# A graph layer's edge loop: its small transfers and index copies made in batches of eight, four and two groups

## The reference, cut to what matters

```
h   = relu(layernorm(x))
msg = relu(concat(h[src], h[dst], w) @ W1 + b1) @ W2 + b2     # one row for each edge
agg = segment_max(msg, dst)                                   # 0 where a node has no edge
x   = x + relu(concat(h, agg) @ U1 + c1) @ U2 + c2
h   = relu(layernorm(x))
x   = x + relu(h @ root + segment_sum(proj[src, rel_type], dst) + bias)
```

## Time and profile before

| what | value |
|---|---|
| time, median of 3 runs | 8358.6 us (8357.57 to 8365.55) |
| span of the one profiled execution | 10613.5 us |
| busy in it: PE / PEld / DVE / ACT / POOL | 6874.5 / 5005.1 / 4445.3 / 959.0 / 6076.6 us |
| first layer's edge loop in it | 151.3 to 5486 us |
| second layer's edge loop in it | 5630.5 to 10581 us |

### The profile page before, as it was taken

One profiled execution on the slowest core, in us unless ns is written; L12 is line 12 of the kernel. 1 busy time (PEld: TensorE's weight loads), 2 busy tenths in 40 slices (PEclk: granted clock), 3 DMA queues, 4 the chain that ended last, 5 costly groups with the idle time before them and its releaser, 6 DMA issues. The chain is left out here.

```text
span 10613.5 us, 125396 instructions
## 1 busy us (share of the span) xinstructions
PE 6874.5 (65%) x29078; PEld 5005.1 (47%) x29078; DVE 4445.3 (42%) x10997; ACT 959.0 (9%) x1738; POOL 6076.6 (57%) x6284
## 2 busy tenths in 40 slices
PE   5767767677677776767675666555656655565656
PEld 3444444444444444444444555444545545454545
DVE  5444444444444444444453343334433433433434
ACT  2100100001000101000021000000000000000001
POOL 2555555555555555555535666666666666666665
PEclk8777777777777777777787777777777777777777
DMA  5222222222222222222232111111111111111112
GB/s 150 74 73 74 72 73 72 73 74 74 73 71 73 72 74 71 74 71 73 72 80 56 42 41 42 42 42 41 42 41 42 41 42 41 42 41 42 41 42 58
DMA packets 415228, 646.13 MB, mean 61 GB/s; under 512 B 128130, under 2 KB 232010, under 8 KB 414451
## 3 DMA queue, kind: packets, MB, share of 16 engines
q0 software_dynamic: 200704, 411.44, 15.7%
q1 hardware_dynamic: 214482, 234.24, 7.6%
HBM read 617.04 MB, written 28.13 MB: 61 GB/s over the span
## 5 line engine op out<-in xcount | busy, mean ns | idle before, releaser
L575 POOL DMA_INDIRECT G<-p_tab,idxs x3136 | 2984.3, 952 | 2441.4 <-DVE idxs L661 1463.1
L1065 POOL DMA_INDIRECT hT<-h_tab,idxs x3136 | 3090.7, 986 | 1849.4 <-issue 911.9
L1082 PE MATMUL psA<-S,hT 128*128 128x256 f32 x6272 | 2131.4, 498 | 1748.4 <-DVE S L1149 1374.1
L1082 PEld LDWEIGHTS psA<-S,hT 128*128 128x128 f32 x6272 | 1490.2, 250 | 2079.1 <-issue 935.2
L678 DVE TENSOR_TENSOR_SCAN R<-mk,R,psM 128x512 f32<-128x512 bf16 x784 | 998.5, 1274 | 1671.2 <-issue 760.0
L603 PE MATMUL psM<-Z,w 128*128 128x512 f32 x1568 | 1115.0, 801 | 855.3 <-ACT Z L649 712.0
L1159 DVE TENSOR_TENSOR aggT<-psV,aggT 128x64 f32 x784 | 174.8, 223 | 2889.2 <-remote 1451.7
L619 PE MATMUL psE<-E,O 128*128 128x64 f32 x6272 | 1025.8, 319 | 406.7 <-DVE E L689 338.3
L1092 PEld LDWEIGHTS psV<-A,V 128*128 128x128 f32 x6272 | 1007.9, 231 | 411.9 <-issue 175.6
L619 PEld LDWEIGHTS psE<-E,O 128*128 128x128 f32 x6272 | 973.2, 237 | 484.2 <-DVE E L689 390.4
L1092 PE MATMUL psV<-A,V 128*128 128x64 f32 x6272 | 969.1, 308 | 273.5 <-ACT A L1110 144.9
(11 more groups left out here) (86 smaller groups left out, 2611.9 us busy)
## 6 DMA issues: line engine op xcount, KB each, us to landing
mk<-marks SPq DMA_DIRECT2D x392, 256.0 KB
G<-p_tab,idxs POOLq DMA_INDIRECT x3136
pl<-marks SPq DMA_DIRECT2D x392, 128.0 KB
hT<-h_tab,idxs POOLq DMA_INDIRECT x3136
Qw<-q_tab SPq DMA_DIRECT2D x784, 32.0 KB
p_tab<-pq SPq DMA_DIRECT2D x14, 448.0 KB, 3.1
q_tab<-pq SPq DMA_DIRECT2D x14, 448.0 KB, 4.1
oh<-in_w SPq DMA_DIRECT2D x392, 4.0 KB
```

Source lines behind the costliest of these rows:

```text
L575: pool.indirect_dma_start(G[:, s, j, :], None, p_tab, bass.IndirectOffsetOnAxis(ap=idxs[:, s, j:j + 1], axis=0)).then_inc(gathered[s], 16)
L1065: pool.indirect_dma_start(G[:, s, j, :], None, h2_tab, bass.IndirectOffsetOnAxis(ap=idxs[:, s, j:j + 1], axis=0)).then_inc(l1_gathered[s], 16)
L1082: ins = nc.tensor.matmul(psA[:, b, 0:NB * W], G[:, s, j, :], S[:, b, j, :, :].rearrange("p b w -> p (b w)"), start=j == 0, stop=j == GT - 1)
```

## The change

A pass of the loop now holds 16 groups (GPB) instead of 8; 49 passes in all. Rings of 8 slots (RING) stay for `G`, `Qw` and `oh`. In `max_edges`:

- `marks` come for eight groups at once, in two buffers, ordered eight groups ahead; `pl` and `mk` are as large as before in all.
- SP loads eight row numbers at once and then brings four windows and the weights of four groups together (`quad`), once PE has used the four groups whose places they take.
- `indices` copies the indices of eight groups with one instruction, in every eighth step, behind that step's `scan`. `idx_ready` counts eights.
- `onehot` forms two groups with one instruction (64 x 1024 elements).
- `E` is formed for two groups with one instruction (`lasts`), ahead of `picks`.
- DVE loads eight row numbers at once for `add`.
- PE, ACT and POOL do the same work with fewer waits. POOL still issues four indirect transfers for each group.

```diff
+GPB = 16
+RING = 8
+QUAD = 4
...
+        def windows(eng, kind, table, at, n):
+
+            _, rows = nc.values_load_multi_w_load_instructions(
+                table[0:1, bass.ds(at, n)], engines=[kind], min_val=0, max_val=NP,
...
+            return rows
...
-                E = sb("E", [P, 2, GT, W], fp32)
-                pl = sb("pl", [WQ, GPI // 2, HALF], bf16)
-                mk = sb("mk", [P, GPI // 2, HALF], bf16)
-                idxs = sb("idxs", [P, GPI, GT], i32)
+                E = sb("E", [P, 2, 2 * GT, W], fp32)
+                pl = sb("pl", [WQ, GPB // RING, OCT], bf16)
+                mk = sb("mk", [P, GPB // RING, OCT], bf16)
+                idxs = sb("idxs", [P, GPB, GT], i32)
...
+                        def marks_in(k, h):
+
+                            sp.dma_start(pl[:, h, :], marks[0, bass.ds(k * GE, OCT)].partition_broadcast(WQ)
+                                         ).then_inc(places_loaded[h], 16)
+                            sp.dma_start(mk[:, h, :], marks[1, bass.ds(k * GE, OCT)].partition_broadcast(P)
+                                         ).then_inc(masks_loaded[h], 16)
+
+                        def quad(i, s, rows, tails):
+                            k, r = GPB * i + s, s % RING
+
+                            if there(k - RING):
+                                sp.wait_ge(z_done, k - RING + QUAD)
+                                sp.nop(nofuse=True)
+                            for n in range(QUAD):
+                                sp.dma_start(Qw[0:W, r + n, :], q_tab[bass.ds(rows[r + n], W), :]).then_inc(windows_loaded[s // QUAD], 16)
...
+                            sp.dma_start(oh[WQ:WQ + 1, r:r + QUAD, :].rearrange("p a e -> p (a e)"),
+                                         row(w)[:, bass.ds(k * GE, QUAD * GE)]).then_inc(windows_loaded[s // QUAD], 16)
...
+                            quad(i, s, rows, tails)
+                            if isinstance(k, int) and k == 0:
+                                marks_in(0, 0)
+                            quad(i, s + QUAD, rows, tails)
+                            if not (isinstance(k, int) and k + RING >= NGRP):
+
+                                if there(k - RING):
+                                    sp.wait_ge(scanned, k + 1)
+                                    sp.nop(nofuse=True)
+                                marks_in(k + RING, 1 - s // RING)
...
-                            pool.wait_ge(idx_ready, k + 1)
-                            pool.nop(nofuse=True)
-                            if there(k - GPI):
-                                pool.wait_ge(z_done, k - GPI + 1)
+                            k = GPB * i + s
+                            if s % RING == 0:
+                                pool.wait_ge(idx_ready, (GPB // RING) * i + s // RING + 1)
+                                pool.nop(nofuse=True)
+                            if there(k - RING):
+                                pool.wait_ge(z_done, k - RING + 1)
                                 pool.nop(nofuse=True)
...
+                        def indices(i, h):
+
+                            s = h * RING
+                            k = GPB * i + s
+                            if there(k - GPB):
+                                for n in range(s, s + RING):
+                                    dve.wait_ge(gathered[n], 16 * GT * i)
+                            dve.nop(nofuse=True)
+                            nc.vector.tensor_copy(idxs[:, s:s + RING, :].rearrange("p s j -> p (s j)"),
+                                                  idx0[:, bass.ds(k * GT, RING * GT)]).then_inc(idx_ready, 1)
...
-                            nc.vector.tensor_scalar(oh[0:WQ, s, :], pl[:, s // 2, b * GE:(b + 1) * GE], place[0:WQ, 0:1], None,
+                            nc.vector.tensor_scalar(oh[0:WQ, r:r + 2, :].rearrange("p a e -> p (a e)"),
+                                                    pl[:, s // RING, r * GE:(r + 2) * GE], place[0:WQ, 0:1], None,
                                                     ALU.is_equal).then_inc(onehot_ready, 1)
...
+                        def lasts(k, r):
+
+                            if there(k - 4):
+                                dve.wait_ge(picked, k - 2)
+                            dve.nop(nofuse=True)
+                            nc.vector.tensor_tensor(E[:, r // 2, :, :], lane[:, :].unsqueeze(1).to_broadcast([P, 2 * GT, W]),
+                                                    relL[:, bass.ds(k * GT, 2 * GT)].unsqueeze(2).to_broadcast([P, 2 * GT, W]),
+                                                    ALU.is_equal)
...
                         def step(i, s):
-                            k = GPI * i + s
-                            if not (isinstance(k, int) and k + HOT >= NGRP):
-                                onehot(i + (s + HOT) // GPI, (s + HOT) % GPI)
-                            if not (isinstance(k, int) and k + AHEAD >= NGRP):
-                                indices(i + (s + AHEAD) // GPI, (s + AHEAD) % GPI)
+                            k = GPB * i + s
+                            if s % RING == 0:
+                                skip = 3 if isinstance(k, int) and k == 0 else 0
+                                dve.nop(nofuse=True)
+                                got = windows(dve, mybir.EngineType.DVE, win, k - 3 + skip, RING - skip)
+                                for n in range(skip, RING):
+                                    rows[s + n] = got[n - skip]
+                            if s % 2 == 0 and not (isinstance(k, int) and k + HOT >= NGRP):
+                                onehot(i + (s + HOT) // GPB, (s + HOT) % GPB)
                             if there(k - 1):
-                                scan(i - (s == 0), (s + GPI - 1) % GPI)
+                                scan(i - (s == 0), (s + GPB - 1) % GPB)
+                            if s % RING == 0 and not (isinstance(k, int) and k + RING >= NGRP):
+                                indices(i + s // RING, 1 - s // RING)
                             if there(k - 2):
+                                if s % 2 == 0:
+                                    lasts(k - 2, (s + 2) % 4)
                                 picks(k - 2, s % 2)
                             if there(k - 3):
-                                add(k - 3, (s + 1) % 2)
+                                add(k - 3, (s + 1) % 2, rows[s])
```

More of the change, by code:

```diff
@@ L499, in _, with rounds @@
                         pool.sem_clear(s)
+        def windows(eng, kind, table, at, n):
+            _, rows = nc.values_load_multi_w_load_instructions(
+                table[0:1, bass.ds(at, n)], engines=[kind], min_val=0, max_val=NP,
+                skip_runtime_bounds_check_because="a window starts at a node and is moved no further than the last row")
+            return rows
         def max_edges(tag, again, wide=False):
             WQ = W + wide
+            BLKS = NGRP // GPB
+            OCT = RING * GE
+            assert NGRP % GPB == 0 and BLKS >= 3
+            def rounds(eng, step):
+                for s in range(GPB):
+                    step(0, s)
+                with eng.Fori(1, BLKS - 1) as i:
+                    for s in range(GPB):
+                        step(i, s)
+                for s in range(GPB):
+                    step(BLKS - 1, s)
             with ExitStack() as ph:
                 sb, ps = tensors(ph, tag)
-                G = sb("G", [P, GPI, GT, D], fp32)
-                Qw = sb("Qw", [WQ + 1, GPI, D], fp32)
-                oh = sb("oh", [WQ + 1, GPI, GE], fp32)
+                G = sb("G", [P, RING, GT, D], fp32)
+                Qw = sb("Qw", [WQ + 1, RING, D], fp32)
+                oh = sb("oh", [WQ + 1, RING, GE], fp32)
                 Z = sb("Z", [P, 2, GE], fp32)
@@ L563, in _ @@
-                        sweep(sp, step)
+                            rows = windows(sp, mybir.EngineType.SP, win, k, RING)
+                            tails = windows(sp, mybir.EngineType.SP, row(last), k, RING) if wide else None
+                            quad(i, s, rows, tails)
[5 more added lines that the diff above has]
+                                    sp.wait_ge(scanned, k + 1)
+                                    sp.nop(nofuse=True)
+                                marks_in(k + RING, 1 - s // RING)
@@ L565, in _ @@
+                        rounds(sp, step)
                     @block.gpsimd
@@ L705, in _ @@
                         dve.wait_ge(place_ready, 1)
-                        for s in range(HOT):
-                            onehot(0, s)
+                        onehot(0, 0)
                         dve.wait_ge(consts_loaded, 48)
@@ L721, in step @@
                                 picks(k - 2, s % 2)
                             if there(k - 3):
-                                add(k - 3, (s + 1) % 2)
-                        sweep(dve, step)
-                        scan(ITERS - 1, GPI - 1)
+                                add(k - 3, (s + 1) % 2, rows[s])
```

(4 more changed lines are left out.)

126 lines of the change are left out of this document (50 added, 76 removed).

## The result

The changed kernel takes 8445.9 us (median of 4 runs, 8444.0 to 8459.9), the kernel before beside it 8358.7 (4 runs, 8357.6 to 8365.6): ratio 1.0106 [1.0094, 1.0119], 87.2 us slower. The forecast, 8384, had the sign and 25 of these 87 us; its range ended at 8420.

What follows compares the result with a forecast made beforehand. POOL's indirect transfers, 1.25 us each and 5.0 us a group, were taken to set the pace of both loops. To 8358.6 us came +25 for longer one-hot holds and 0 for all else: 8384 us, range 8335 to 8420.

Steps and rivals of the forecast that it cites:

- The ledger: POOL's idle time in both loops: 2250 us of real waits, taken off the 10613.5 us span, leave 8363 us.
- the waits belong to the profiled execution: Both loops: in timed runs POOL hardly ever waits; the 2250 us of waits occur only in the profiled execution.
- E was put at nothing: DVE's E for two groups: 0.67 us a pair, hidden behind POOL's 5.0 us a group; no holds assigned to it.
- the one-hots' base: First loop's gathers: 19 us of extensions by single one-hots, 26 us if POOL were always at work.
- the memset's 5: The gather of 5.80 us beside the 10.6 us memset, read as the large case of the hold: 4.9 us.
- square law: Gathers beside one-hots: cost grows with hold length squared; pairs cost 1.8 to 2.8 times singles, +21 to +48 us.
- its 0.37 us: A gather beside a one-hot: POOL shut out for 0.09 + 0.28 us from the one-hot's start; pairs 0.70 to 0.88.
- Marks: Marks loaded for eight groups: 1.5 MB at once, landing near 12.8 us, wanted after 30 us; 0 us.
- The index copy: DVE's index copy by eights: 779 copies become 98, saving DVE 120 us off the path; slack 27 us, 0 us.
- Rival 1: First loop's gathers: longer holds fall where DVE doesn't touch the port; 8358 us, bounds 8342 to 8375, chance 0.38.
- Rival 2: POOL waits in timed runs; the deeper index lead removes it: 8301 to 8244 us; chance 0.12 including small gains.
- Rival 3: A late window or mark stalls PE: 98 us if once in eight groups at 1 us, 8457 us; chance 0.04.

Runs made afterwards that it cites:

- b3: The kernel before, unchanged, profiled again in the short condition: gathers of the first loop mean 965 ns; timed 8376.6 us beside e7b.
- e5: The changed kernel with E for two groups reading `lane` from PSUM instead of SBUF: 10156.6 us, 0.9576 of the kernel before, long condition.
- e6: The changed kernel with one-hot pairs formed by a slower three-input operation, one input in PSUM: 10106.6 us, 0.9530 of the kernel before, long condition.
- e4: The changed kernel with one-hots and E for one group again: 10137.4 us, 0.9540 of the kernel before, long condition.
- a1: The changed kernel, unchanged, run again in the long condition: 10192.7 us, 0.9612 of the kernel before.
- e2: The changed kernel with one-hots for one group again, E still in pairs: 10165.4 us, 0.9569 of the kernel before, long condition.
- e7b: The changed kernel with one-hot pairs and E pairs each taking one input from PSUM, short condition: 8318.6 us, 0.9931 of the kernel before.

## Why the prediction came out short

**The ledger was right as arithmetic and wrong as a reading.** Span less POOL's waits is the time of the short condition, to 0.05%, and in after POOL waits 2.7 us, with gaps of 0.305. But "the waits belong to the profiled execution" was false. They belong to a condition that timed runs have too. The conclusion that POOL sets the pace holds for the result, since the time to be predicted was of the short one.

**The step that failed: E was put at nothing, and the one-hots' base was too small.** The prediction gave all holds to the one-hots: 19 us of them (24 less the memset's 5), scaled to 26, and a factor of 1.8 to 2.8. Each gather that is held ends one of two fixed times after the end of one DVE instruction (below), so its excess can be put to that instruction. Counted over the mean of the gathers that nothing stretches (946.0 ns in b3, 943.6 in after), in us:

| held by | before (long) | b3 (short) | after (short) | after less b3 | in the prediction |
|---|---|---|---|---|---|
| one-hots | 9 | 42 | 85 | +43 | 26 to 51, +25 |
| E | 11 | 11 | 67 | +56 | nothing |
| memset's gather | 5 | 5 | 0 | -5 | 0 |

*E.* It is the larger part, +56 us, nearly the 62 us that the forecast fell short. In the trace that the prediction had, E already held about half of it; it read one gather beside a one-hot and gave the rest to the one-hots too, without a reason. e5 and e6 show both parts by leaving out: 58 us for E and 62 for the one-hots, of 114. Here the Trainium skill had the missing half on the page the prediction cited ("SBUF — State Buffer", section "SBUF: two separate sides"): the pair of ports is also locked by a DVE operation with two inputs in SBUF, against a GpSimd operation that reads SBUF. The trace agrees: E is such an operation, the gather reads `idxs`, and with `lane` in PSUM its share goes.

*The one-hots' base* was counted where POOL was standing. In the long condition the index copy comes right behind the one-hot and POOL waits for that copy, so POOL is mostly not at a gather's start while a one-hot runs. Scaling by POOL's busy share, 3920 of 5313, takes the two as independent, and they aren't: in before, 318 of 778 one-hots start in one of POOL's waits, which fill 28% of the time, and 75 are under way when a gather begins; in b3, without waits, 425 of 780 are. The base is 42 us, not 26. The factor for them, 85/42 = 2.0, is in the prediction's range.

**The factor, and what a hold is.** In the long condition pairs over singles give 2.5 (e4 to a1); in the short one 152 of after stand to 50 of b3, 3.0. The prediction had 1.8 to 2.8 by a square law on a hold read from one pair of rows, and took the lower end; the one-hots alone have 2.0, E alone 6. Sorted by where the DVE instruction starts, seen from the start of the gather that overlaps it alone, the records of both kernels give one law (ns):

| instruction, kernel | starts at | gathers | mean excess | its end less the excess |
|---|---|---|---|---|
| one-hot of 2, after | -550 to -500 | 42 | 87 | 125 |
| | -350 to -300 | 15 | 286 | 126 |
| | -150 to -100 | 57 | 483 | 124 |
| | -50 to 50 | 14 | 0 | |
| | 200 to 250 | 7 | 142 | 820 |
| | 350 to 400 | 11 | 288 | 821 |
| | 550 to 900 | 148 | 0 | |
| E of 2, after | -400 to -350 | 76 | 160 | 127 |
| | 50 to 100 | 30 | 468 | |
| | 300 to 350 | 38 | 0 | |
| one-hot of 1, b3 | -350 to -300 | 38 | 24 | 126 |
| | -150 to -100 | 73 | 224 | 125 |
| | 0 to 350 | 185 | -1 | |
| | 400 to 450 | 9 | 77 | 824 |

A gather wants something that DVE holds at two moments, 0.125 and 0.82 us after its start. If a one-hot that began at least 0.1 us ahead of the gather (an E: 0.02) is still running at the first, the gather waits for its end. At the second it waits for a one-hot that began less than 0.47 us into it, never for an E. The row "50 to 100" of E is a mixture. In 24 of its 30 gathers the index copy of eight groups runs across the first moment, as in the timeline above, and 23 of them wait to the end of the E behind it, 0.61 us; the six without the copy wait for nothing. In e5, with the same copy there and `lane` in PSUM, 14 such gathers lose 0.014 to 0.022 us, to the copy's end. So the index copy in eights isn't free: together with E it brings 14 of E's 67 us.

These rules give all but some 3 us of what is held in after and in b3. They are of these two kernels, these two instructions and the short condition. In the long one they leave more open: in e2 five gathers beside an E that starts 0.32 us after them are held 0.85 us (the longest 1803 ns), and in e6 15 us of 56 follow neither moment. The hold also goes the other way. A one-hot that starts 0.55 to 0.7 us into a gather ends 1.455 us after the gather's start wherever in that stretch it began (44 in after), 0.715 and its usual 0.74; in b3 15 of them end at 1.19, 0.715 and 0.475.

For the first moment a one-hot's useful length is its own less 0.22 us. A single one-hot has a quarter of a microsecond left (0.475 - 0.22), a pair has 0.51. For the second, a single one that starts 0 to 0.34 us into the gather is over before 0.82, a pair is not. Met at any phase of 1.25 us, the one-hots would cost 784 x (0.25^2/2 + 0.125^2/2) / 1.25 = 24 us as singles and 392 x (0.51^2/2 + 0.39^2/2) / 1.25 = 65 as pairs; E by the first moment alone 784 x 0.27^2/2 / 1.25 = 23 and 392 x 0.53^2/2 / 1.25 = 44. Together 47 and 109, an estimate with a factor of 2.3; measured 50 and 152.

By kind the estimate is up to twice off either way: 24 and 65 against 42 and 85 for the one-hots, 23 and 44 against 11 and 67 for E. That rest is phase, which the law of squares leaves out: 57 pairs of one-hots start in the costliest 50 ns, and 118 of the 392 E pairs start 0.72 to 0.9 us into a gather, from where 0.67 us reach past the first moment of the next and 0.42 would not. The change set both the length and the phase, and no run in the short condition separates them.

The prediction read its 0.37 us (0.09 ahead and 0.28 of excess) as the whole hold and found that it "ended before the one-hot did". It did not: that one-hot's end, 0.38 us after the gather's start, less 0.28 is 0.10, near the first moment. The Trainium skill's rule ("SBUF — State Buffer", section "SBUF: two separate sides") that GpSimd is blocked until the end of DVE's instruction plus some 115 ns agrees in this, that the excess follows that end one for one; whether 115 ns come on top can't be read, since the records show when a gather ends and not when it is let go.

**The sum of the account.** Gathers of the first loop: 3112.0 - 3025.0 = 87.0 us; time: 87.2. That agreement is closer than the figures bear: the two executions' median gathers differ by 3 ns, 9 us over the loop, and by the holds alone it is 152 - 55 = 96 us, 9 more than measured. With the one-hots' base of b3 and its low factor the prediction would have come to 42 x 0.8 = +34, with the high one to 42 x 1.8 = +76. So the right base for the one-hots alone doesn't reach 87 us; E's +56 has to come in.

**The other steps.** One-hot pairs took 757 ns, below the 0.81 to 0.99 given, E pairs 671 as said; groups of DVE instructions in the loop of after:

```profile
L689 DVE TENSOR_SCALAR oh<-pl,place 64x1024 f32<-64x1024 bf16 x392 | 296.9, 757 | 179.5 <-issue 137.2 <-PE psZ L610 42.3
L709 DVE TENSOR_TENSOR E<-lane,relL 128x512 f32<-128x512 f32 x392 | 263.1, 671 | 0.0
```

Marks land after 5.0 and 7.2 us of the 30 they had. No wait of POOL names the windows, the marks or the longer body, and e7b, which has them all, shows no cost of them. The index copy, put at nothing as well, has its part in the 14 us above.

**The rivals.** Rival 1 (no change) falls by the mean of 992. Rival 2, a gain by the deeper lead, does not occur where POOL never waits. In the long condition there is a gain (-4%), but that the lead brings it isn't shown: a lead of seven brought none in the first loop. Rival 3 falls by POOL's waits.

## What to carry to other kernels

Where one engine sets the pace without waiting, look at what stretches its instructions: the spread of their durations beside those of its neighbours, not the idle time. Go through all stretched instructions and ask of each what ran beside it; one pair of rows showed the one-hot here and hid E. A hold can cost more than in proportion to its length: half as many instructions of 1.6 times the length cost two times as much (one-hots) and six times (E). One operand moved to PSUM took E's away. And a base is only good in the condition for which it is used: a profile in which the pacing engine waits showed its holds too small.

## What the runs showed of the hardware

- The same kernel took 8358 to 8384 us or 10448 to 10629 us (one chip showed 8370 to 8384 and 10612 to 10629), and the order of the versions turns round between the two. In the long condition ACT starts a median 3.9 us after PE's last matmul of a group instead of 0.04.
- DVE with its inputs in SBUF stretched a gather of 0.944 us by up to 0.62 in the changed kernel (most 1563 ns) and by up to 0.86 in e2 (most 1803 ns); a longer operation with an input in PSUM (1.27 us) left the mean at 943 and 946.
- In after and b3, a gather of 0.94 us is delayed at two moments, 0.125 us (one-hot or E) and 0.82 us (one-hot) after its start, to the end of the DVE instruction less that constant, the same to a few ns in both kernels. One-hots begun 0.55 to 0.7 us into a gather are delayed in turn, to end at 0.715 us plus their own length.
- Most gathers beside the 10.6 us memset are not held: five in a row took 944 to 947 ns in before, and the sixth took 5.80 us; in the changed kernel eight took 940 to 945 ns and the ninth 1265. What held the one of 5.80 us isn't shown, so the memset is no large case of the same hold, as the prediction took it.
